# Outputs of the first twelve groups are started inside the drain of the second layer, and their part of the decision tree is worked four steps earlier in its own buffers

## The reference

```
h = h + _L1_attn_ref(_layernorm(h), qkv_w, qkv_b, out_w, out_b, rel_pos_emb)
h = h + _L1_ffn_ref(_layernorm(h), weights_in, weights_out)

def _L1_ffn_ref(inputs, weights_in, weights_out):        # 21 nodes, depth 11
    all_logits = einsum('bsd,nd->bsn', inputs, weights_in)
    def step(prev_idx, _):
        sel = clip(prev_idx, 0, max_index)
        logits = take_along_axis(all_logits, sel[..., None], axis=-1)[..., 0]
        new_idx = clip(2 * sel + 1 + (logits > 0), 0, max_index)
        return new_idx, (logits, new_idx)
    ...
    act = gelu(logits)                                    # of the nodes on the path
    coeff = einsum('dbs,dbsn->bsn', act, one_hot(node_idx))
    return einsum('bsn,nd->bsd', coeff, weights_out)
```

## Time and profile before

| | |
|---|---|
| median of 3 runs | 1703.57 us (1697.69 to 1705.97) |
| the profiled execution, its own time | 1706.06 us |
| its span from first to last instruction | 1704.2 us |
| PE busy | 1575.2 us (92%) |
| DVE busy | 1252.1 us (73%) |
| ACT busy | 1121.1 us (66%) |
| mean granted TensorE clock | 0.961 of full |

### The profile page before, as it was taken

How to read it: one execution, slowest core, us unless ns; L and a number is a source line. 1 busy time by engine, 2 the same in 40 slices (tenths; PEclk the granted TensorE clock), 3 DMA queues, 4 the chain that set the end, 5 groups by cost and what they waited for, 6 DMA issues and landing times. The chain is left out here.

```text
span 1704.2 us, 58821 instructions
## 1 busy us (share of the span) xinstructions
PE 1575.2 (92%) x18950; PEld 1433.3 (84%) x18950; DVE 1252.1 (73%) x2845; ACT 1121.1 (66%) x3086; POOL 807.2 (47%) x1457
## 2 busy tenths in 40 slices
PE   4999999997479999999999999588999999999987
PEld 4888888886369999999999999477888888888873
DVE  5999999996875555555555555277899998888976
ACT  3999999995364334334333343287899999998961
POOL 5677777762022222322222322455677777766620
PEclk9999999999689999999999999689999999999987
DMA  3422222222117888888889888377788888888844
GB/s 93 104 72 71 72 73 70 73 67 54 54 56 217 259 258 257 254 259 257 254 258 256 258 255 224 97 195 200 205 226 227 223 223 223 224 217 218 224 121 148
DMA packets 350675, 302.35 MB, mean 177 GB/s; under 512 B 44669, under 2 KB 315730, under 8 KB 350610
## 3 DMA queue, kind: packets, MB, share of 16 engines
q1 hardware_dynamic: 333346, 263.01, 54.9%
q0 software_dynamic: 16032, 37.51, 8.9%
q10 hardware_dynamic: 1232, 1.00, 0.2%
HBM read 208.27 MB, written 93.15 MB: 177 GB/s over the span
## 5 line engine op out<-in xcount | busy, mean ns | idle before, releaser
L1094 ACT ACTIVATE prob<-ps_s,b1s 128x256 f32<-128x256 f32 x426 | 179.1, 472 | 345.3 <-PE ps_s L1061 307.0
L989 POOL DMA_INDIRECT xs<-zn_d,idx x71 | 68.9, 970 | 366.2 <-PE ps_t L1025 364.6
L1061 PE MATMUL ps_s<-xhi,w1hi_c 128*128 128x256 f32 x852 | 236.8, 296 | 1.6 <-ACT xhi L1087 1.6
L1061 PE MATMUL ps_s<-xhi,w1lo_c 128*128 128x256 f32 x852 | 227.1, 284 | 0.0
L1036 PE MATMUL ps_v<-probT,prob 128*128 128x192 f32 x852 | 208.3, 326 | 0.0
L1036 PE MATMUL ps_k<-probT,prob 128*128 128x192 f32 x852 | 208.1, 326 | 0.0
L417 PE MATMUL ps_q<-xT,wqk_c 128*128 128x128 f32 x1536 | 203.7, 285 | 3.4 <-ACT xT L661 2.9
L417 PEld LDWEIGHTS ps_q<-xT,wqk_c 128*128 128x128 f32 x1536 | 194.3, 200 | 7.4 <-ACT xT L661 3.6
L640 ACT ACTIVATE kT<-ps_q,halves 128x128 f32<-128x128 f32 (+1 forms) x512 | 172.3, 364 | 3.3
L1061 PEld LDWEIGHTS ps_s<-xhi,w1hi_c 128*128 128x128 f32 x852 | 164.2, 193 | 2.0 <-ACT xhi L1087 2.0
L589 ACT ACTIVATE prob<-score 128x768 f32<-128x768 f32 (+1 forms) x128 | 149.0, 1164 | 23.6 <-DVE score L744 21.8
(11 more groups left out here) (233 smaller groups left out, 4146.2 us busy)
## 6 DMA issues: line engine op xcount, KB each, us to landing
rel_d<-rpad SPq DMA_DIRECT2D x64, 864.0 KB
relb<-rel_d SPq DMA_DIRECT2D x64, 768.0 KB, 5.2
probT<-w2h SPq DMA_DIRECT2D x71, 576.0 KB, 4.2
score<-w1h SPq DMA_DIRECT2D x71, 384.0 KB, 3.3
score<-w1h SPq DMA_DIRECT2D x142, 192.0 KB, 4.4
ys_d<-ys SPq DMA_DIRECT2D x71, 192.0 KB, 5.0
tok<-b2h SPq DMA_DIRECT2D x71, 96.0 KB, 5.0
posb<-base_d SPq DMA_DIRECT2D x128, 48.0 KB
```

Of the source, the lines that this page charges most:

```text
L1061: last = pe.matmul(dst, w, x, start=(k == 0), stop=(k == len(terms) - 1))
L1094: last = act.activation(hT[b][:, c, :], ps_s[:, j, (c % 2) * BLK:(c % 2) * BLK + BLK], ACT.Gelu, bias=b1s[b][:, c:c + 1])
```

## The change

`fg` and `fr` get buffers of their own. The two fills of `fc` and `fr` on POOL go from steps 66 and 67 to step 10. DVE does part 0's `scaled` behind step 64, `reach` behind 65 and 66 (before: behind 68 and 69), `coefficients`, `last_reach` and `leaves` all behind step 68 (before: behind 70 and 71). ACT does part 0's Gelu behind step 67 (before: 69). Behind the steps 68 to 73 two groups' `decode_turn` and `decode_turned` are put on PE and ACT, and a step later their products and outputs. Groups 12 to 15 and part 1 of the tree come after step 73.

```diff
--- before.py
+++ after.py
@@ -441,6 +441,8 @@
                     b, t = st.two("pt"), st.tile("pt")
                     if u == 0:
                         pe.wait_ge(S["p_sb"], upto(t))
+                        if l == 1 and isinstance(t, int) and t == NT - 1:
+                            pe.wait_ge(F_["cT_sb"], 2)
 
                         after(pe, S["pt_sb"], npt * t)
                         if l == 0:
@@ -1438,7 +1440,7 @@
         def in_tiles(buf, width):
             return buf[:].rearrange("p h s -> p (h s)")[:, 0:NT * width].rearrange("p (t n) -> p t n", n=width)
 
-        fg, fr = in_tiles(relb[1], NODES), in_tiles(rpad[0], NODES)
+        fg, fr = sb("fg", [128, NT, NODES])[:], sb("fr", [128, NT, NODES])[:]
         LEAVES = NODES - 10
         prod = in_tiles(relb[0], LEAVES)
         cT4 = [relb[0][:].rearrange("p h s -> p (h s)")[:, 1024 + 128 * p:1152 + 128 * p] for p in range(2)]
@@ -1451,12 +1453,15 @@
         EARLY = 12
         PARTS = [slice(0, 4 * EARLY), slice(4 * EARLY, NT)]
         turn_bank = [ps_k, ps_q]
+        LASTSTEP = NT + max(AGES[1].values()) - 1
+        INSIDE = 2 * (LASTSTEP - 67)
+
+        def drained(n):
+            return range(2 * (n - 68), 2 * (n - 67)) if 68 <= n <= LASTSTEP else ()
 
         def decode_pool(pool, n):
-            if n == 66:
+            if n == 10:
                 pool.memset(fc[:], 0.0).then_inc(F_["fc"], 1)
-            if n == 67:
-                pool.wait_ge(M[1]["rst"][0], 16 * (NT // 2))
                 pool.memset(fr, 1.0).then_inc(F_["fr"], 1)
 
         def decode_gelu(act, part):
@@ -1473,7 +1478,7 @@
         def decode_turn(pe, m):
             p = m % 2
             pe.wait_ge(F_["ready"], 1 if m < EARLY else 2)
-            pe.wait_ge(L[1]["pt_sb"], 3 * NT)
+            pe.wait_ge(L[1]["pt_sb"], 3 * (NT - 1) if m < 2 else 3 * NT)
 
             after(pe, F_["cT_sb"], m - 1)
             pe.transpose(turn_bank[p][:, 0:128], fc[:, 4 * m:4 * m + 4, :].rearrange("p k n -> p (k n)"), ident[:])\
@@ -1506,7 +1511,6 @@
                 self.dve.wait_ge(L[1]["y_ok"], tiles)
                 scale = rsza[:, self.ts].rearrange("p (t o) -> p t o", o=1)\
                     .to_broadcast([128, tiles - self.ts.start, NODES])
-                self.dve.wait_ge(L[1]["s_rd"], NT)
                 self.dve.tensor_tensor(self.fg, self.lg, scale, ALU.mult).then_inc(F_["scaled"], 1)
 
             def children(self, t, lo, n, side):
@@ -1542,6 +1546,7 @@
                 k, c = self.ch.link, small[:, 1, self.ts]
                 last, g = self.fc[:, :, LAST:NODES], self.fg[:, :, LAST:NODES]
                 pr = prod[:, self.ts, :]
+                self.dve.wait_ge(L[1]["s_rd"], NT)
                 self.ch.done()
                 k(self.dve.tensor_tensor(pr, self.fr[:, :, 10:NODES], self.fg[:, :, 10:NODES], ALU.mult))
                 k(self.dve.tensor_reduce(c, pr, AX.X, ALU.add))
@@ -1602,9 +1607,16 @@
 
             @block.tensor
             def _(pe):
-                pe_steps(pe, 1)
-                decode_turn(pe, 0)
-                for m in range(NM):
+                def behind(n):
+                    for m in drained(n - 1):
+                        decode_product(pe, m)
+                    for m in drained(n):
+                        decode_turn(pe, m)
+                pe_steps(pe, 1, behind)
+                for m in drained(LASTSTEP):
+                    decode_product(pe, m)
+                decode_turn(pe, INSIDE)
+                for m in range(INSIDE, NM):
                     if m + 1 < NM:
                         decode_turn(pe, m + 1)
                     decode_product(pe, m)
@@ -1612,13 +1624,14 @@
             @block.scalar
             def _(act):
                 def behind(n):
-                    if n == 69:
+                    if n == 67:
                         decode_gelu(act, 0)
+                    for m in drained(n):
+                        decode_turned(act, m)
                 act_steps(act, 1, behind)
-                for m in range(NM):
+                decode_gelu(act, 1)
+                for m in range(INSIDE, NM):
                     decode_turned(act, m)
-                    if m == 1:
-                        decode_gelu(act, 1)
 
             @block.vector
             def _(dve):
@@ -1635,25 +1648,27 @@
                 early, late = Decode(dve, ch, 0), Decode(dve, ch, 1)
 
                 def behind(n):
+                    if n == 64:
+                        early.scaled()
+                    if n == 65:
+                        early.reach(LEVELS[0:2])
+                    if n == 66:
+                        early.reach(LEVELS[2:4])
                     if n == 68:
-                        early.scaled()
-                        early.reach(LEVELS[0:2])
-                    if n == 69:
-                        early.reach(LEVELS[2:4])
-                    if n == 70:
                         early.coefficients(LEVELS)
-                    if n == 71:
                         early.last_reach()
                         early.leaves()
+                    for m in drained(n - 1):
+                        decode_output(dve, m)
                 dve_steps(dve, 1, behind)
-                for m in range(NM):
-                    if m == 1:
-                        late.scaled()
-                        late.reach(LEVELS)
-                    if m == 3:
-                        late.coefficients(LEVELS)
-                        late.last_reach()
-                        late.leaves()
+                late.scaled()
+                for m in drained(LASTSTEP):
+                    decode_output(dve, m)
+                late.reach(LEVELS)
+                late.coefficients(LEVELS)
+                late.last_reach()
+                late.leaves()
+                for m in range(INSIDE, NM):
                     decode_output(dve, m)
 
 
```

## The result

The changed kernel takes 1707.49 us (median of 20 runs, 1701.21 to 1712.28), the kernel before 1701.88 (20 runs, 1697.66 to 1706.35): a ratio of 1.0032, 95% interval [1.0019, 1.0045], so 5.4 us slower (3.2 to 7.7; the medians themselves lie 5.6 apart). Forecast were 1709 us and a loss of 5.5 on the profiled execution. The profiled execution spans 1707.5 us, 3.3 more than that of before.

What follows compares the result with a forecast made beforehand. It took no engine to set the pace when the drain begins, but DMA, with the last tile's exponential on the path. 6.5 + 2.2 - 4.3 = +4.4, plus 1.1 for the clock, made +5.5: 1709 us, range 1697 to 1719.

Steps and rivals of the forecast that it cites:

- the clock's share: Drain: +1.1 us added to the sum in case TensorE's clock comes back one step later (+3.0, given a good third).
- the hold: Steps 68 and 69: the last exponential waits on ACT for part 0's coefficients, leaves, turns and two copies, 5.7 us.
- Fills in step 10: POOL's two fills ahead of a gather: 3.0 us under DVE's idle time and the gather's lead, taken as 0.
- Tree work in steps 64 to 66: Part 0's early DVE work, about 3.7 us: taken as 0, covered by waiting; rival that it isn't, 1713, chance 0.10.
- Two table switches: Around part 0's Gelu: step 68's exponential 2.8 us late, the last subtraction 0.1 to 1.4 late, taken as 0.8.
- The last exponential behind groups 0 and 1: Largest term, on ACT: copies of two groups precede the last exponential, 5.7 us later; +6.5 with the table switches' 0.8.
- faster, because the last exponential isn't held: Rival: part 0 ready by the end of step 68's sums, wait under 1 us, -11 us, 1692; chance 0.08.
- Last exponential to last addition: To the last tile's addition: six groups +8.2, PE's own work at the upper clock -5.0, Gelu moved -1.0; together +2.2.
- my main case: TensorE's clock comes back to the upper level with the first pair of groups, then two at 2.0 us, four at 1.05.
- Last addition to end: From the last tile's addition to the end: 25.3 us where it was 29.6, -4.3, last four groups at the lower clock.
- The clock: TensorE's clock in the drain, worth 10 us each way; rivals: up or back at once 1698 (0.16), down throughout 1720 (0.15).

Runs made afterwards that it cites:

- before_loads: The kernel before plus one useless Gelu behind step 67, so with the changed kernel's two table loads alone: 1703.65 us, ratio 1.0025 to the kernel before.
- tree_only: The changed kernel with part 0's tree still early but all groups put back behind step 73: 1702.63 us, ratio 1.0013 to the kernel before.
- no_switch: The changed kernel with the exponential in place of Gelu for part 0 (other output values), so without the two table loads: 1702.14 us, ratio 1.0007 to the kernel before.
- first_no_switch: The changed kernel with groups one step later and the exponential in place of part 0's Gelu, so no table loads behind step 67: 1702.17 us, 1.0011 to before.
- exp_first: The changed kernel with all groups started one step later, so no group's copy precedes the last exponential: 1706.50 us, ratio 1.0036 to the kernel before.
- hold_more: The changed kernel with part 0's coefficients computed four times behind step 68, 5.5 us more DVE work: 1709.79 us, ratio 1.0061 to the kernel before.
- fills_64: The changed kernel with the two POOL fills behind step 64 in place of step 10: 1704.43 us, ratio 1.0015 to the kernel before.
- after_warm: The changed kernel with useless matmuls in TensorE's pauses of the drain: 1698.63 us, ratio 0.9993 to the kernel before.
- first_warm: exp_first with useless matmuls in TensorE's pauses (four, four and eleven): 1695.70 us, ratio 0.9979 to the kernel before.
- tree_warm: tree_only with four useless matmuls ahead of the turned probabilities of each of tiles 62 and 63: 1698.65 us, ratio 1.0001 to the kernel before.
- before_warm: The kernel before with four useless matmuls ahead of tile 63's turned probabilities: 1698.15 us, ratio 0.9998 to the kernel before.
- first_warm2: first_warm with tile 62's four useless matmuls in another bank, no longer waiting for the last relative addition, and two, not four, for tile 63: 1699.86 us, ratio 0.9988 to before.

## Why the prediction was right, and where it was not

- **The total.** Right: +5.4 us by the ratio for +5.5. Along the chain, against the marks of before by the clock of the span: last exponential 6.8 later (forecast 6.5), last tile's addition 7.4 (8.7), end of the span 3.3 (4.4, or 5.5 with the clock's share). But some terms describe this execution rightly and could not be shown to be causes, and that the sum fits is in part luck: the table loads, taken as 0.8, measured 4.3, and the hold, taken as 5.7, gave nothing when it was taken away. By the ratios the way from before to the changed kernel is: the loads alone +4.3 (before_loads, uncertainty 2.8), part 0's tree and the fills with them -2.0 (tree_only, 3.7), the groups +3.2 (changed, 3.3). Only the first step is clear of its uncertainty. Without the loads all the rest of the change costs 1.2 us (no_switch, -0.9 to 3.2).
- **Fills in step 10, taken as 0.** The place was misjudged: DVE waited for the gather for 5.75 us in step 12. I had weighed 3.0 us of fills against an idle time of 2.4 and the gather's lead. Of the net price the runs tell only that it is small; the ratios allow 0 to about 7 us, the additions' own times point to 1 or 2. It stays open.
- **Tree work in steps 64 to 66, taken as 0.** Bounded, not isolated: tree_only, which has this work, the fills and the loads, is 2.0 us under before_loads, which has the loads alone (uncertainty 3.7). DVE still idled 1.96 and 0.94 us for the relative scores in steps 66 and 67. In the chain of the changed kernel `scaled` stands on the path in step 64, but PE waited only 0.16 us for the sums behind it.
- **Two table switches, taken as 0.8.** This term was mis-sized. Three pairs of kernels that differ in the loads (before and before_loads, no_switch and changed, first_no_switch and exp_first) give 4.3 us each, together 4.3 with an uncertainty of about 2. As forecast were each load's 1.28 us and the exponential of step 68, 3.7 us behind the last copy. What of it reaches the last subtraction was not: this is 1.2 us later than before by the clock of the span, but the last relative scores were added 1.5 us sooner than before. Counted from that addition the subtraction is 2.7 us late (6.98 us behind it for 4.26), and the last exponential 8.3, which is these 2.7 and the hold's 5.65. The page ScalarE: Activation LUTs of the Trainium skill (What ACT_TABLE_LOAD costs) would have 1.38 us of drain more per switch; the trace agrees on the load and disagrees on the drain: 0.02 us at most lie on either side of a load (1643.37 + 1.28 to the Gelu at 1644.66). Where the 4.3 are lost stays open in part. Up to the last exponential two of the three pairs show 2.7 and 3.2 us of direct delay. My next theory was that PE's pause of 3.3 to 3.8 us puts its clock down sooner. The profile of before_loads shows a drain in which that cost nothing, but it is the execution with the highest clock of its twelve, and the mean clocks of all three pairs go with the theory. The profiled drains differ by 0 to 0.9 us within the three pairs, and can't decide it: one of them is the slowest execution of its kernel, another among the quickest.
- **The last exponential behind groups 0 and 1, +5.7.** The mechanism and its size in the trace are right (5.65 us from the subtraction's end), and hold_more shows that a longer hold is paid nearly in full (4.3 of 5.6 us in the drain, 4.9 by the ratios). Its value as a cause was not borne out: taken away together with one step's delay of the groups, it brings nothing (exp_first against the changed kernel +0.7 us, first_no_switch against no_switch +0.7, uncertainty 3.4 and 3.3). In the profiles two things take its place. PE's own work at the lower level fills part of that stretch. And what is gained up to the last tile's addition (2.2 us, and 4.5 from no_switch to first_no_switch) is lost behind it, where two groups more stand (2.2 and 4.3). The rival "faster, because the last exponential isn't held" did not come about: part 0's last leaf is ready at 1658.4, not before 1653, and the kernels in which nothing holds that exponential lose 6.1 (exp_first) and 1.9 us (first_no_switch) where it had a gain of 11.
- **Last exponential to last addition, +2.2.** Measured +0.6 (22.7 for 22.1), with the clock back at 1671, behind the first pair of products, as in my main case. It moves with the clock rather than with the hold: 22.7 and 22.9 us at a granted clock of 0.73 (changed, hold_more), but 26.4 and 26.5 at 0.61 and 0.60 (no_switch and fills_64, which have the hold too), 25.7 and 27.4 at 0.55 and 0.56 (exp_first and first_no_switch, which don't).
- **Last addition to end, -4.3.** Measured -4.1. Groups 12 and 13 ran at the lower level as forecast (1.65 us a product), 14 and 15 for the most part (2.38 us for both; two take 2.93 at the lower level and 1.56 at the upper). Not foreseen was a wait of 1.22 us for an output buffer's store.
- **The clock.** I called it what the prediction fails most easily by. The runs with filled pauses bear out that the pauses cost: 6.6 and 9.7 us less for the two kernels with groups in the drain. Whether the groups in the drain are a loss because of the clock is not shown. While the pauses stay, changed and exp_first are 3.2 and 3.9 us over tree_only (uncertainty 3.3 and 3.6), and with them filled, after_warm and first_warm are 1.4 and 3.7 us under tree_warm (4 each). But these two have useless matmuls in the tail too, and tree_warm has none there.

## What to carry to other kernels

Moving work forward into a stretch that waits pays only if it brings no new wait with it. Here part 0's Gelu took two table loads with it, to a place where PE waits for ACT's next exponential, and they are the one part of the loss that the runs tell clearly: 4.3 us, where their place in the profile had suggested 0.8. So put an activation of another kind where no other engine waits for ACT, and look for what a change does to the pauses of TensorE ahead of its work, not only for what it delays. A hold that stands on the chain isn't worth its length: before you remove it, ask what else ends just short of it, and what your way of removing it puts elsewhere. And before you rest a theory on one profile, see where its execution lies among the others of its kernel, by its time and by its granted clock.

## What the runs showed of the hardware

- The time for which the clock stayed at 0.50 after a pause differed widely: 3 us (tree_warm, 1642.5 to 1645.5, PE busy all along), 13 (tree_only, 1640 to 1653, PE busy for 11.6), 30 (exp_first, 1646 to 1676, busy for 28.1), 37 (before_loads, 1639 to 1676, busy for 33.1). I can't tell from these traces how soon work brings it back.
- The same drain of 57.7 us stands in one execution of the kernel before at a granted clock of 0.74, and in one of before_loads at 0.68. Between these two executions the earlier fall of the clock (1639 for 1654, with the last exponential at 1645.5 and 1652.5) cost nothing.
- Filling one pause with matmuls of no use doesn't keep the clock up over the next. In before_warm it stayed at 1.00 for 8 us behind the last exponential and fell behind a pause of 2.24 us; in first_warm2 a stretch of 2.6 us with 0.73 us of work was followed by 0.52. In after_warm, four of them behind a semaphore that came late took 5.33 us at the lower level.
- A table load took 1.28 us in the drain of each of the 14 traces, with at most 0.02 us on either side. Only in tree_only and tree_warm the activation behind one load comes 0.96 us later, and there it waits for `scaled` on DVE.
